# Attention: the value products of two units of keys stand together in TensorE's program

## The reference

```python
logits = jnp.einsum('bhqd,bhkd->bhqk', q, k) * scale
logits = logits + (1.0 - mask)[None, None, :, :] * big_neg   # causal
attn = jax.nn.softmax(logits, axis=-1)
out = jnp.einsum('bhqk,bhkd->bhqd', attn, v)
```

## Time and profile before

| | us |
|---|---|
| median of three runs | 4936.78 (4935.09 to 4944.33) |
| the profiled execution's own time | 4933.36 |
| its span | 4931.6 |
| attention's stretch (925 to 1870 holds 31 of its 32 groups) | 889 to 1902 |

### The profile page before, as it was taken

One profiled execution on the slowest core, in us unless ns is written; L12 is line 12 of the kernel. 1 busy time (PEld: TensorE's weight loads), 2 busy tenths in 40 slices (PEclk: granted clock), 3 DMA queues, 4 the chain that ended last, 5 costly groups with the idle time before them and its releaser, 6 DMA issues. The chain is left out here.

```text
span 4931.6 us, 117903 instructions
## 1 busy us (share of the span) xinstructions
PE 4195.4 (85%) x49696; PEld 2649.1 (54%) x49696; DVE 3070.1 (62%) x5364; ACT 2309.5 (47%) x3824; POOL 2409.9 (49%) x1569
## 2 busy tenths in 40 slices
PE   6399968699999996739997799879999999997798
PEld 5255545233333333625555544367777777875576
DVE  4511145687888884641116466479899899997574
ACT  1021124366666663101115367667667776763233
POOL 1034344222222223113432245479999899997553
PEclk6599989799999998769998899989999999998899
DMA  6132256655555544422323236643333333333552
GB/s 214 39 83 44 37 181 225 110 88 88 88 88 88 88 71 158 144 78 46 49 36 102 85 143 259 233 124 98 94 88 100 94 101 88 98 98 105 215 202 80
DMA packets 325609, 548.93 MB, mean 111 GB/s; under 512 B 55104, under 2 KB 221168, under 8 KB 325072
## 3 DMA queue, kind: packets, MB, share of 16 engines
q1 hardware_dynamic: 291328, 487.10, 36.5%
q0 software_dynamic: 24576, 34.10, 4.4%
q10 hardware_dynamic: 9168, 20.09, 1.1%
HBM read 326.98 MB, written 212.86 MB: 109 GB/s over the span
## 5 line engine op out<-in xcount | busy, mean ns | idle before, releaser
L2331 POOL TENSOR_TENSOR s_hc<-s_hs,s_ct 128x1024 f32<-128x1024 f32 x512 | 1213.5, 2384 | 91.6 <-DVE s_hs L2310 77.1
L2310 DVE TENSOR_TENSOR_SCAN s_hs<-s_dA,s_psB 128x1024 f32<-128x1024 f32 x512 | 1167.3, 2285 | 126.3 <-PE s_psB L2244 63.8
L2244 PE MATMUL s_psB<-s_diag,s_duT 128*32 128x128 f32 x32768 | 962.7, 274 | 53.2 <-issue 28.2
L2244 PEld LDWEIGHTS s_psB<-s_diag,s_duT 128*32 128x32 f32 x32768 | 909.6, 111 | 157.5 <-issue 108.4
L1229 DVE CUSTOM_DVE_ANT_0 a_masked<-a_psM,a_later 128x1024 f32<-128x1024 f32 (+7 forms) x1024 | 734.0, 753 | 213.7 <-PE a_psM L1277 201.5
L1213 ACT ACTIVATE a_wt<-a_psE 128x512 f32<-128x512 f32 (+1 forms) x1216 | 627.4, 578 | 356.1 <-PE a_psE L1301 346.5
L2187 ACT ACTIVATE s_dA<-s_dlt,s_aneg 128x1024 f32<-128x1024 f32 x512 | 587.8, 1148 | 343.5 <-DVE s_hs L2310 339.6
L1192 POOL TENSOR_SCALAR_AFFINE_SELECT a_wt<-a_wt 128x512 f32<-128x512 f32 x256 | 162.3, 634 | 769.9 <-ACT a_wt L1213 769.9
L1277 PE MATMUL a_psM<-a_kst,a_qst 96*128 96x512 bf16 (+3 forms) x1536 | 421.8, 337 | 99.9 <-DVE a_mx L1229 68.0
L1301 PE MATMUL a_psE<-a_qst,a_kst 99*128 99x512 bf16 (+3 forms) x1536 | 413.7, 331 | 4.1 <-ACT a_wt L1213 2.4
L2167 ACT ACTIVATE s_diag<-s_ident,s_bt 128x128 f32<-128x128 f32 x972 | 322.2, 388 | 13.6 <-ACT s_ys L2176 13.5
(11 more groups left out here) (305 smaller groups left out, 5939.4 us busy)
## 6 DMA issues: line engine op xcount, KB each, us to landing
s_dlt<-dd SPq DMA_DIRECT2D x128, 512.0 KB, 4.5
a_qst<-qs SPq DMA_DIRECT2D x192, 128.0 KB, 6.7
a_kst<-ks SPq DMA_DIRECT2D x192, 128.0 KB, 7.2
yd<-s_ys ACTq DMA_DIRECT2D x33, 512.0 KB, 2.7
vs<-a_va SPq DMA_DIRECT2D x8, 2048.0 KB, 6.9
a_va<-vs SPq DMA_DIRECT2D x32, 512.0 KB, 10.4
zsd<-s_zs SPq DMA_DIRECT2D x32, 512.0 KB, 7.5
ucd<-s_uc SPq DMA_DIRECT2D x8, 2048.0 KB, 13.3
```

Of the source, the lines that this page charges most:

```text
L2244: ins = pe.matmul(psB[s][DG * m:DG * (m + 1), c * P:(c + 1) * P], duT[j % 2][:, c, DG * r:DG * (r + 1)], diag[:, place(NB * g + m, u), c, ...
L2310: dve.tensor_tensor_scan(hs[k % 2][:, :], dA[k % 2][:, :], psB[s][:, :], 0.0, ALU.mult, ALU.add).then_inc(scanned, 1)
L2331: pool.tensor_tensor(hc[NB * (g % 2) + r][:, :], hs[k % 2][:, :], ct[:, g, :], ALU.mult).then_inc(weighed, 1)
```

## The change

The values of two units now stand one behind the other, in every odd unit k, in the middle of its shares: those of unit k-3 and then those of unit k-2. The rule for units that start a half is gone. The last two units of all are done behind the loop, as before.

```diff
                     shares = SHARES[k % NU]
-                    early = (k - LAG) % NU not in FIRSTS
                     for i in range(len(shares)):
                         score(k, i)
-                        if k >= LAG and i == (len(shares) // 2 if early else len(shares) - 1):
+
+                        if k > LAG and k % 2 and i == len(shares) // 2:
+                            values(k - LAG - 1)
                             values(k - LAG)
                 for k in range(GROUPS * NU - LAG, GROUPS * NU):
                     values(k)
```

## The result

| | before | after |
|---|---|---|
| median, us | 4940.12 (4 runs, 4935.09 to 4944.33) | 4996.50 (4 runs, 4981.08 to 5000.94) |
| ratio | | 1.0109, 95% interval 1.0083 to 1.0135 |
| span of the profiled execution | 4931.6 | 4991.1 |
| first to last turning of the maxima | 951.6 | 1006.3 |
| distance between two turnings at full clock (one group) | 30.67 | 31.66 |

The stage itself is 54.7 us longer; that is nearly all of the span's 59.5. It comes in two parts. Each group is 0.99 us longer: 31 x 0.99 = 30.7 us. And 16 of the 31 distances are longer still, 14 of them by about 1.6 us and two by 2.65: the other 24 us.

The account below looks back on a forecast made before the run. TensorE looked like the bound, but not alone: it and VectorE wait for each other over two psM buffers. 31 groups x 1.05 = 32.6 us on 4933.4 give 4966, median 4969; own range 4950 to 4988, 8 in 10 4940 to 4996.

Parts of the forecast that it names:

- V6's 0.57: Scores S8.0 to S9.3: values of unit 6 no longer lie under VectorE's reciprocal; 6.40 us becomes 6.97, +0.57 a group.
- V8's 0.55: Scores S9.3 to S11.3: values of unit 8 no longer fill the wait for the third M1024; +0.55 us a group.
- The sum for a group: All six stretches of a group in attention: +1.05 us, with the pairs' saving of 1.44 and lost cover of 2.49.
- S11.3 to S2.0: From scores of unit 11 to unit 2: pair saves 0.24, but S1.0 gets its buffer later; 4.70 us becomes 4.64, -0.06.
- The saving of a pair: Two value products together pay the way into and out of the 32-column layout once: 0.24 us saved a pair.
- A pair saves nothing: Rival: each value product pays its 0.24 us wherever it stands; 5014 us. Chance 0.06, together with the clock.
- the fourth M256: Sign, in S8.0 to S9.3: TensorE waits some 0.8 us for VectorE at this product of the maxima.
- the third M1024: Sign, in S9.3 to S11.3: TensorE waits some 0.8 us for VectorE at this product of the maxima.
- the clock: Rival: granted clock falls to 1.2 GHz for a tenth of the stage, 71 us on top; chance 0.06 with pair saves nothing.
- It cancels: Rival: lost cover is 1.4 us a group instead of 2.5; 4937 us, give or take 10. Chance 0.07.
- TensorE is simply the bound: Rival: the waits are absorbed and 32 x 1.44 = 46 us go; 4891 us. Chance 0.08.
- The last group: Has no maxima beside it; saving of up to 1.4 us against bursts on ScalarE: 0, give or take 3.

Follow-up runs that it names:

- e2: Kernel before with only V8 (values of unit 8) moved to V9: 4955.4 us, ratio 1.0034; group 31.22 us.
- e3: Kernel before with V0, V2, V4 and V10 moved to their neighbours, V6 to V9 standing alone: 4929.8 us, ratio 0.9989; group 30.55 us.
- e5: Changed kernel with VectorE's reciprocal behind the 22nd maximum of a group instead of the 25th: 4950.1 us, ratio 1.0035 to the kernel before.
- e4: Changed kernel with scores S8.3 (unit 8) computed four times, ahead of the wait for the fourth M256: 4954.3 us, ratio 1.0043 to the kernel before.
- e9: Kernel before with only V6 moved to V7, and scores S8.3 computed four times: 4937.8 us, ratio 1.0012; group 31.02 us.
- e1: Kernel before with only V6 (values of unit 6) moved to V7: 5001.6 us, ratio 1.0137; group 31.02 us.
- e8: Changed kernel with scores S11.3 (unit 11) computed four times, at a place without a wait for VectorE behind it: 5024.6 us (one run).

## Why the prediction was right, and where not

- **The direction and the mechanism were right**: V6 and V8 lay under VectorE's work, and moved out of it they cost more than six pairs save. e2, e3 and e5 show it apart. How the cost was divided, V6's 0.57 and V8's 0.55, holds only with both moved: V6 alone costs 0.35.
- **The sum for a group was right**: +1.05 forecast, +0.99 measured. By stretch, forecast and measured after: S8.0 to S9.3 6.97 and 6.96; S9.3 to S11.3 6.59 and 6.59; S11.3 to S2.0 4.64 and 4.62; to S4.0 3.64 and 3.64; to S6.0 4.35 and 4.34; to S8.0 5.54 and 5.51.
- **The saving of a pair was right**: V6+V7 keeps the next product off for 1.43 us, where 1.00 + 0.58 alone would be 1.58, and the way in is paid once less. 0.86 + 0.58 = 1.44 was forecast. V10+V11, two of 512, keep it off for 1.86 = 0.86 + 1.00 (1441.86 to 1443.72). "A pair saves nothing" is refuted.
- **The signs named in advance**: the waits of about 0.7 to 0.8 us at the fourth M256 (0.64) and the third M1024 (0.73) are there; VectorE idles 0.99 us behind V6+V7 and 1.05 behind V8+V9 ("more than 1" was forecast), and the second V of a pair starts 0.88 us after the first (0.86 forecast).
- **The step that failed is the clock.** I had it as a rival, wrote that the granted clock should stay at 1.00, "I see no reason for it in rows with waits of nearly that size", and gave it, together with another case, 0.06. The clock fell to 0.50 in 16 of 31 groups. That was wrong reasoning: it judged the waits by their size alone. The waits of before, 0.28 and 0.47 us, stood on either side of V6; now two waits of 0.64 and 0.24 us stand close together with only 256- and 128-column products between them. e4 and e9 show that filling this stretch stops most falls, and e2 that a wait of 0.62 us among wide products brings none. The falls were 24 us of the stage's 54.7. Its size, 71 us, was off as well: the fall lasts for one pair and its surroundings, 1.6 us of loss, in about every second group. So the time came out at 4996.5 and not 4969, above the forecast's own range (4950 to 4988) and half a us above the range of 8 in 10 (to 4996), with the cause of the excess on the list at too small a chance.
- "It cancels" and "TensorE is simply the bound" fell with the group's 31.66 us.
- The last group was put at 0, give or take 3. From the last turning to the start of the last value product the kernel before takes 31.4 us (1869.2 to 1900.6) and the changed one 34.9 (1920.5 to 1955.4): 3.5 of the 4.8 us by which the span grew outside the stage.
- Left open: why the fall is in 16 of 31 groups of the changed kernel, in 24 of e1 and in 25 of e8, whose stretches are the same in the order of work.

## What to carry to other kernels

A product that pays a fixed price for its place may still be free, if it stands where the engine would wait: before gathering such products, look up for each what it covers, and gather only those that cover nothing. Read the order of time of the engine that answers, for the stretch between two buffers, and count what each side can do without the other. And when a change makes new waits on TensorE, look at the granted clock of the windows around them: here two waits of 0.64 and 0.24 us were followed by a fall that cost the group about 1.6 us more, in 16 of 31 groups.

## What the runs showed of the hardware

- More work made the program faster: with 0.66 us of repeated products in each group, in a wait, the granted clock fell in 3 groups and not in 16, and the stage went from 1006.3 us to 983.5. The same work elsewhere made it 1038.4 us, with 25 falls (one run).
- A wait of 0.62 us among 512-column products (e2) brought no fall; waits of 0.64 and 0.24 us around 256- and 128-column products did.
- A pair of value products at 1.2 GHz holds the next product off for 2.72 us, at 2.4 GHz for 1.43.
- Products of the same 32-column layout following each other pay no way in or out between them: 0.86 us a bundle in the scan, and in attention V10+V11 hold the next product off for 1.86 us where each alone takes 1.10.
